# One fused kernel on one core: the experts' down-projection in plain fp32 with tokens on the partitions, and a reordered front and hand-over

## The reference

```python
x = x + xattn0(ln(x), ctx)      # softmax of tri-linear scores, 4 x 256 x 256, then z = [c, a, c*a, c*q2c] @ W_l.T + b_l
x = x + experts(ln(x))          # E = 8 experts, H = 256, top 2 by logits
x = x + xattn1(ln(x), ctx)      # 16 heads of 8, W_q W_k W_v W_o, b_o
x = x + fp8_layer(ln(x))        # rounded to fp8, 128 x 128

def experts(x):
    logits = x @ Wg;  top_vals, top_idx = top_k(logits, 2)
    weights = one_hot(top_idx) * softmax(top_vals)
    for e in range(8):
        u, v = x @ W1[e], x @ W2[e]
        out += ((u * sigmoid(u) * v) @ W3[e]) * weights[..., e]
```

## Time and profile before

| | us |
|---|---|
| median of 3 runs | 230.06 |
| the profiled execution | 230.04 |
| its span, first to last instruction | 228.2 |
| PE, DVE, ACT, POOL busy | 188.1, 167.8, 138.3, 123.9 |
| share of the ending chain: PE, DVE, POOL, ACT, issue | 49%, 13%, 13%, 12%, 9% |
| mean granted PE clock | 0.938 |

### The profile page before, as it was taken

How to read it: one execution, slowest core, us unless ns; L and a number is a source line. 1 busy time by engine, 2 the same in 40 slices (tenths; PEclk the granted TensorE clock), 3 DMA queues, 4 the chain that set the end, 5 groups by cost and what they waited for, 6 DMA issues and landing times.

```text
span 228.2 us, 4007 instructions
## 1 busy us (share of the span) xinstructions
PE 188.1 (82%) x1166; PEld 144.7 (63%) x1166; DVE 167.8 (74%) x408; ACT 138.3 (61%) x273; POOL 123.9 (54%) x141
## 2 busy tenths in 40 slices
PE   5758896795998999999989868789999999886130
PEld 4546795373776788788868657567876887563120
DVE  3775766169697878869874699688988998845764
ACT  2282742974654565645672458988789798665452
POOL 4368464994966999859995246254223232203502
PEclk9999769599999999999999999999999999999755
DMA  6991000000750503203900000000000000000002
GB/s 221 370 408 50 4 0 0 0 0 3 237 134 3 177 10 95 92 0 95 274 0 4 0 0 3 0 0 3 1 4 0 0 0 1 0 3 0 1 0 92
DMA packets 6434, 13.04 MB, mean 57 GB/s; under 512 B 1024, under 2 KB 2048, under 8 KB 6160
## 3 DMA queue, kind: packets, MB, share of 16 engines
q1 hardware_dynamic: 4688, 11.83, 15.3%
q10 hardware_dynamic: 1728, 1.00, 1.4%
HBM read 10.17 MB, written 0.56 MB: 47 GB/s over the span
## 4 chain that ended last, share of the span: by engine, by line
PE 49%; DVE 13%; POOL 13%; ACT 12%; issue 9%; ACTq 2%; DVEq 0%; POOLq 0%
POOL hids L306 7%; PE banks L1353 6%; PE bank L1334 5%; PE bank L1365 5%; PE bank L1106 4%; PE bank L1108 3%; PE bank L1107 3%; PE banks L1106 3%; PE banks L1108 3%; POOL cpT L316 3%; PE banks L1107 3%; DVE negm L973 2%; PE bank L1280 2%; ACT raw L601 2%; POOL att L267 2%
## 5 line engine op out<-in xcount | busy, mean ns | idle before, releaser
L306 POOL TENSOR_TENSOR hids<-attT,hids 128x512 fp32r<-128x512 f32 x32 | 40.9, 1296 | 10.4 <-ACT hids L517 10.2
L973 DVE TENSOR_REDUCE negm<-bank 128x2 f32<-128x512 f32 x64 | 41.9, 687 | 5.3 <-PE bank L1334 3.9
L354 POOL TENSOR_TENSOR wx<-raw,const 32x256 fp32r<-32x256 f32 x32 | 19.5, 608 | 39.3 <-DVE raw L963 32.1
L601 ACT ACTIVATE raw<-banks 128x1024 f32<-128x1024 f32 x32 | 32.5, 1021 | 2.7 <-PE banks L1353 2.4
L517 ACT CAST hids<-attT 128x512 fp32r<-128x512 f32 x32 | 19.9, 621 | 18.7 <-DVE attT L894 10.8
L889 DVE SCALAR_TENSOR_TENSOR att<-att,bank 128x512 f32<-128x512 f32 x32 | 21.9, 684 | 12.0 <-ACT att L511 12.0
L1334 PE MATMUL bank<-wx 128*128 128x512 f32 x64 | 24.9, 430 | 2.0 <-DVE wx L983 1.5
L511 ACT ACTIVATE att<-bank 128x512 f32<-128x512 f32 x32 | 18.8, 594 | 9.2 <-PE banks L1108 7.7
L1106 PE MATMUL bank<-xT,wx 128*128 128x512 f32 x48 | 19.7, 411 | 0.8 <-DVE att L889 0.7
L1108 PE MATMUL bank<-xT,wx 128*128 128x512 f32 x48 | 19.1, 398 | 0.0
L1107 PE MATMUL bank<-xT,wx 128*128 128x512 f32 x48 | 19.0, 396 | 0.0
(11 more groups left out here) (220 smaller groups left out, 463.8 us busy)
## 6 DMA issues: line engine op xcount, KB each, us to landing
rwb<-routing SPq DMA_DIRECT2D x8, 512.0 KB, 4.1
raw<-in_w SPq DMA_DIRECT2D x1, 2048.0 KB, 11.2
wx<-negm SPq DMA_DIRECT2D x1, 2048.0 KB, 8.8
raw<-in_w SPq DMA_DIRECT2D x1, 1024.0 KB, 9.6
xs<-in_x SPq DMA_DIRECT2D x2, 256.0 KB, 3.1
ctxT<-in_ctxT SPq DMA_DIRECT2D x1, 512.0 KB, 5.3
ctx<-in_ctx SPq DMA_DIRECT2D x1, 512.0 KB, 7.1
wl<-in_wl SPq DMA_DIRECT2D x1, 256.0 KB, 7.6
```

The source lines that it names most:

```text
L306: pool.tensor_tensor(hids[:, p, 1, k, :], hid[:, p, k, :], plain(hids[:, p, 0, k, :]), ALU.subtract).then_inc(S["hid_lo"], 1)
L601: act.activation(probs[:, g % 2, 2 * r:2 * r + 2, :, :].rearrange("p h k q -> p (h k q)"), pair[r][:, :], ACT.Exp, scale=ATT_SCALE).then_i ...
L973: dve.tensor_reduce(negm[:, g % 2, r // 2, c0:c0 + QUAD + 1:QUAD], bk[1 + r % 2][:, :].rearrange("p (h k) -> p h k", h=2), AX.X, ALU.max, ...
```

## The change

The experts. `down(n)` uses the hidden tile itself (fp32, not split) as the stationary operand, 128 tokens at a time, and W3 as loaded as the moving operand: eight fp32 products of 128 columns, and the result has tokens on the partitions. So the rounding and the remainder of `hid` go, the split of W3 goes, `weigh` becomes four operations that scale by `rw` (one number for each partition) and add to `xs`, and the accumulation on POOL, the spreading of the routing weights, and both turnings back go. ACT uses Silu in place of tanh, so one DVE product in `hidden` goes; the routing's exp becomes a tanh.

The front. The eight row scalings of the attention are shared by DVE (first tile of a batch) and POOL (second tile, now a tensor_tensor); PE runs 5 + 3 + 3 products with the identity between them (`keep_warm`), and `WARM_UP` is 4. `b_l` is added on POOL ahead of the scalings. `turned(1)` and the copy of `cT` for half 0 go to ACT. z is made by halves: `contexted(0)` stands ahead of `queried(1)`. The normed tiles are made on DVE again, V is projected behind z, half one is turned and `up(0)` starts ahead of the turning of half two and of the logits.

The hand-over. `km` has its own tile and is cleared early; projections 0 and 1 run ahead of `up(14)` and `up(15)` in bank 7; `scores(0, 0, 0)` and `(0, 0, 1)` stand ahead of `down(15)`.

```diff
-WARM_UP = 6
+WARM_UP = 4
@@ transfers (SP)
-            for h in range(2):
-                sp.wait_ge(S["rwT_ev"], h + 1)
-                sp.dma_start(rw_d[:, cols], rwT[:, cols]).then_inc(S["rw_out"], 16)
...
-            sp.wait_ge(S["y_ps"], UNITS - G - 1)
+            sp.wait_ge(S["setup"], 1)
+            sp.wait_ge(S["ld_w12"], 16)
             blank = negm[:, :, :, :]...
@@ POOL
+            for h in range(2):
+                pool.wait_ge(S["ln1"], HALVES[h][1])
+                pool.tensor_tensor(xs[:, tiles, :], xs[:, tiles, :], bl..., ALU.add).then_inc(S["bl_added"], 1)
+            for b in range(BATCH):
+                t = TPB * b + 1
                 pool.wait_ge(S["s_rinv"], b + 1)
-                for t in range(TPB * b, TPB * (b + 1)):
-                    pool.tensor_scalar(att[:, t, :], att[:, t, :], rinv[:, t:t + 1], None, ALU.mult)
+                pool.tensor_tensor(att[:, t, :], att[:, t, :], rinv[:, t:t + 1].broadcast_to([P, SEQ]), ALU.mult)
-            w12_lo(0, 1, 2, 3, 4, 5)
-            negative_mean(0, HALVES[0])
-            w12_lo(6)
-            negative_mean(1, HALVES[1])
-            w12_lo(7)
-            for e in range(0, E, 2):
-                pool.tensor_tensor(w3[:, e:e + 2, 1, :], w3raw[:, e:e + 2, :], plain(w3[:, e:e + 2, 0, :]), ...)
+            w12_lo(0, 1, 2, 3, 4)
+            for h in range(2):
+                inverse_deviation(2, h, HALVES[h])
+            pool.wait_ge(S["ln2"], NT)
+            w12_lo(5, 6, 7)
-            for n in range(2, UNITS):
-                hidden_lo(n)
-                if (n - 2) % E and n - 2 < UNITS - 3:
-                    accumulate(n - 2)
@@ ACT
-                    act.activation(tanhs[:, k, :], bk[2 * k][:, :], ACT.Tanh, scale=0.5).then_inc(S["tanh_s"], 1)
+                    act.activation(silus[:, k, :], bk[2 * k][:, :], ACT.Silu).then_inc(S["silu_s"], 1)
-            def hidden_hi(n, k): ...
+            act.activation(spare[:, :], const[:, C_ZERO:C_ZERO + 1], ACT.Silu)     # ahead of the experts
+            act.activation(spare[:, :], const[:, C_ZERO:C_ZERO + 1], ACT.Exp)      # behind them
@@ DVE
             def inverse_sum(b):
                 ...
+                dve.wait_ge(S["s_rinv"], b + 1)
+                dve.tensor_scalar(att[:, TPB * b, :], att[:, TPB * b, :], rinv[:, TPB * b:TPB * b + 1], None, ALU.mult)
             def hidden(n):
-                    dve.scalar_tensor_tensor(gated[:, k, :], tanhs[:, k, :], 1.0, bk[2 * k][:, :], ALU.add, ALU.mult)
-                    dve.tensor_tensor(hid[:, p, k, :], gated[:, k, :], bk[2 * k + 1][:, :], ALU.mult)
+                    dve.tensor_tensor(hid[:, p, k, :], silus[:, k, :], bk[2 * k + 1][:, :], ALU.mult)
             def weigh(n):
-                dve.tensor_tensor(out, bk[4 + n % 2][:, :], rwb[:, e, :], ALU.mult).then_inc(S["y_w"], 1)
+                for t in range(TPH):
+                    tile = h * TPH + t
+                    ins = dve.scalar_tensor_tensor(xs[:, tile, :], bk[4 + n % 2][:, t * P:(t + 1) * P],
+                                                   rw[:, tile, e:e + 1], xs[:, tile, :], ALU.mult, ALU.add)
+            context_added(0)
+            added_moments(0)
+            context_added(1)
+            scaled(2, 0, HALVES[0])
+            added_moments(1)
+            normed_lo(0)
+            scaled(2, 1, HALVES[1])
@@ PE
+            keep_warm(6, 5)
             attention_turned(0)
+            keep_warm(6, 3)
             attention_turned(1)
+            keep_warm(6, 3)
+            attention_turned(2)
             context_to_query(0)
+            queried(0, range(0, 2))
             (q2c products)
-            queried(0)
+            queried(0, range(2, TPH))
+            contexted(0)
             queried(1)
-            for h in range(2):
-                contexted(h)
+            contexted(1)
             def down(n):
-                for k in range(HB):
-                    ins = three(bk[4 + p][:, :], (w3[:, e, 0, k * P:(k + 1) * P], w3[:, e, 1, k * P:(k + 1) * P]),
-                                (hids[:, p, 0, k, :], hids[:, p, 1, k, :]), k == 0, k == HB - 1)
+                for t in range(TPH):
+                    rows = slice(t * P, (t + 1) * P)
+                    for k in range(HB):
+                        ins = pe.matmul(bk[4 + p][:, rows], hid[:, p, k, rows], w3raw[:, e, k * P:(k + 1) * P],
+                                        start=t == 0 and k == 0, stop=t == TPH - 1 and k == HB - 1)
+            up(0)
+            turn("ln2", "xT_ps", 5, 1)
+            logits(0)
+            up(1, (0,))
+            logits_turned(0)
+            up(1, (1,))
+            for n in range(2, UNITS):
+                if n >= UNITS - 2:
+                    for a in range(2):
+                        project(n - UNITS + 2, n - UNITS + 2, 0, a, bank=7)
+                up(n)
+                ...
+                down(n - 2)
             down(UNITS - 2)
-            project(0, 0, 0, 1, early=True)
-            second_half_part(accT[:, HALF:TOK], first=True)
-            second_half_part(yw3)
-            second_half_part(yw[:, 0, :])
-            down(UNITS - 1)
-            project(0, 0, 0, 0, early=True)
-            second_half_part(yw[:, 1, :], last=True)
             for r in range(2):
                 scores(0, 0, r, True)
+            down(UNITS - 1)
-            for a in range(2):
-                project(1, 1, 0, a)
```

More of the change, by code:

```diff
@@ L193, in build @@
         S = {n: sem(n) for n in names}
-        def added(n):
-            return n - n // E
         block = stack.enter_context(nc.Block())
@@ L1013, in dve_batch @@
                         stack_keys(m + 2, (g + 2) % G, first and g < 2)
-                    if first and g == 0:
-                        add_experts(1)
                     if more:
@@ L1115, in turn, with keep_warm @@
                 ins.then_inc(S[out], 1)
+            def keep_warm(bank, count):
+                for _ in range(count):
+                    pe.matmul(bk[bank][:, 0:P], ident, ident, start=True, stop=True)
             pe.wait_ge(S["setup"], 1)
@@ L1178, in _, with queried @@
             ins.then_inc(S["bcol_ps"], 1)
-            def queried(h):
+            def queried(h, tiles=range(TPH)):
                 pe.wait_ge(S["cc_ev"], h + 1)
-                for t in range(TPH):
+                for t in tiles:
                     tile = h * TPH + t
@@ L1214, in _ @@
                 ins.then_inc(S["v_ps"], 1)
-            for h in range(2):
-                turn("ln2", "xT_ps", 4 + h, h)
+            turn("ln2", "xT_ps", 4, 0)
             def logits(h):
@@ L1268, in down @@
-                ins.then_inc(S["y_ps"], 1)
-            def first_half_turned():
-                pe.wait_ge(S["y_acc"], added(E - 1))
-                for t in range(TPH):
-                    ins = pe.transpose(bk[6][:, t * P:(t + 1) * P], accT[:, t * P:(t + 1) * P], ident)
-                ins.then_inc(S["accT_ps"], 1)
-            def second_half_part(src, first=False, last=False):
-                for t in range(TPH):
-                    ins = pe.matmul(bk[7][:, t * P:(t + 1) * P], src[:, t * P:(t + 1) * P], ident,
-                                    start=first and t == 0, stop=last and t == TPH - 1)
-                if last:
-                    ins.then_inc(S["accT_ps"], 1)
@@ L1306, in project @@
-            def project(m, g, b, a, late=None, early=False):
-                if a == 0 and not early:
+                for t in range(TPH):
+                    rows = slice(t * P, (t + 1) * P)
+                    for k in range(HB):
+                        ins = pe.matmul(bk[4 + p][:, rows], hid[:, p, k, rows], w3raw[:, e, k * P:(k + 1) * P],
+                                        start=t == 0 and k == 0, stop=t == TPH - 1 and k == HB - 1)
+                ins.then_inc(S["y_ps"], 1)
+            def project(m, g, b, a, late=None, bank=0):
+                if a == 0:
```

466 lines of the change are left out of this document (180 added, 286 removed).

## The result

| | before | after |
|---|---|---|
| median, us | 230.56 | 224.66 |
| range of the runs, us | 229.29 to 231.51 | 223.94 to 225.35 |
| profiled execution: span, us | 228.2 | 222.0 |
| mean granted PE clock | 0.938 | 0.954 |

The ratio is 0.973, with a 95% interval of 0.969 to 0.977: 2.7% faster, where 5.5% were forecast. 224.66 lies outside the range of 212.5 to 223.5. The spans differ by 6.2 us, the medians by 5.9.

What follows compares the result with a forecast made beforehand. PE was taken to bound the experts' stage, with waits and half clock ahead of it. Front -10.4, stage +3.5, hand-over -6.3, first batch -0.7 gave -13.9; with 1.3 for the clock, -12.6 on 230.04: 217.4 us, range 212.5 to 223.5.

Steps and rivals of the forecast that it cites:

- The experts' stage: From the end of up(0) to the end of down(14): 71.1 us before, 74.6 after, so +3.5.
- DVE has two products [...] hidden either way: Experts, per unit: DVE's products and scale-and-add operations take 2.5 to 2.8 us in a 4.6 us unit, hidden behind PE.
- The forecast is wrong [...] if DVE rather than PE ends the waits in it: Failure sign for the experts' unit, beside a unit over 5 us, up(0) starting after 39, or half clock over 7 us.
- PE's own price: Experts, per unit: eight fp32 products cost 1.78 us, six removed matmuls save 1.39, returning to fp32r costs 0.09.
- rival "slower": Experts' downs: weight loads not hidden, 3.0 us more a unit, 45 us in all, 262 us; chance 0.04.
- The wait for routing: Experts' stage: one wait of PE for routing, 0.5 us within the 74.6.
- The front: Start to the end of up(0): -10.4 us, from 48.77 to 38.4.
- clock not held: Rival: both half-level clock stretches return, or one in the first 12 us from the shorter warm-up; 222.9 us; chance 0.16.
- lesson of L797: Front, row scalings: DVE's SBUF operations are late beside a POOL tensor_tensor; L797 took 1.14 us where L800 took 0.23.
- The rival made of it: Front, port rival: row scalings wait for each other and delay maxima and copies, +2.6, 220.0 us; chance 0.12.
- Hand-over and batch 0: End of down(14) to turn_maxima: 5.1 us for 11.4, -6.3; second attention's first batch: add_experts leaves DVE, -0.7.
- The clock: Allowance of 1.3 us for a half-level stretch of 6.8 us, with PE waiting around 33 to 35 us.

Runs made afterwards that it cites:

- e1: Changed kernel with three hidden buffers instead of two, so hidden(n) waits for down(n-3); 217.05 us, 0.9405 of the kernel before.
- e8: e1 with the second hidden block left out of every down, four products instead of eight, output incomplete; 208.61 us, one run.
- e3: Changed kernel with WARM_UP 6, as before the change, instead of 4; 223.28 us, 0.9687 of the kernel before.
- e6: e1 with both row scalings of a batch on DVE, none on POOL; 216.07 us, 0.9384 of the kernel before.
- e9: e1 plus WARM_UP 6, both row scalings on DVE and seven identity products in the hand-over; 215.53 us, 0.9358 of the kernel before.
- e2: Changed kernel, still two hidden buffers, with down and weigh one unit behind up instead of two; 217.87 us, 0.9459 of the kernel before.
- e7: e1 with seven identity products in PE's waits of the hand-over; 217.10 us, 0.9421 of the kernel before.
- e10: e9 plus b_l added late on POOL (kv in its own tile) and no keep_warm in the front; 214.69 us, 0.9341 of the kernel before.
- e11: e9 with two hidden buffers and down one unit behind up, in place of three buffers; 214.94 us, 0.9331 of the kernel before.
- e5: e1 with b_l added on POOL behind its row scalings and w12_lo(0), kv in its own tile; 217.86 us, 0.9471 of the kernel before.
- e4: Changed kernel without the eleven keep_warm identity products of the front; 224.16 us, 0.9731 of the kernel before.

## Why the prediction was wrong, step by step

**The experts' stage, the step that failed.** "DVE has two products [...] hidden either way" and "without that cover, DVE's 2.8 would still be below PE" compare amounts of work. They were right as amounts (0.687 and four in 1.12 us) and said nothing on the *place* of the wait. For the stage I added up PE's matmuls and put every wait on DVE at nothing, and I missed that `hidden` had got a new one: `y_ps` moved from the writers of the split copies to DVE's product, and that product frees bank 1 for the next up. With the down two units behind, the two form a circle PE up, DVE product, PE down, each once a unit. The unit was 4.97 us, not 4.64. By e1, nine units by 0.45 and 1.8 of the wait for `norm_lo`, 5.8 us of the stage, and 0.7 of the hand-over hang on it: 6.5 us in all. The profiled execution, 223.94, misses the forecast by the same 6.5; what else went wrong (front 1.7, batch 0 0.9 too little) is about made up by what I had priced too high in the stage (1.5) and held back for the clock (1.3). Between the medians the miss is 7.3, since that execution was the fastest of the four. "The forecast is wrong [...] if DVE rather than PE ends the waits in it" was the right alarm, and it went off: the 0.58 at 80.63 and the 2.05 at 106.70 both end with DVE.

**PE's own price was right, a little high.** The down's sixteen records run from 77.84 to 79.54: 1.70 us, where I had 1.78. Behind them the first two fp32r matmuls start 0.31 us apart instead of 0.23, the 0.09 that I had. With e1 the unit is 4.52 against my 4.64 and the stage 73.1 against 74.6. The four products of the earlier trace rows with their fixed identity were a fair stand-in: weight loads are hidden (rival "slower" falls; e8 gives 0.22 again). The wait for routing, 0.5, didn't show.

**The front, 1.7 us short.** The parts came in (z for half one is added at 30.80 instead of 34.86, at full clock from 13.7 on; up(0) at 37.17 instead of 45.41). Three things in it I had priced at nothing. WARM_UP 4 let the clock fall at 10.3 us on the scores: 1.0 us, by e3. I had it only inside the rival "clock not held". `b_l` on POOL was "while POOL is idle": it was, but DVE wasn't. Its normed tiles took 2.09 beside POOL's 1.26 (0.97 more), and a 128 x 1 sum took 1.26 beside the second addition. I had applied's lesson of L797 to the scalings and not to this tensor_tensor ten lines ahead. And the scalings: shared, they cost DVE 0.81 a batch, where both on DVE take 0.62 (e6).

**Row scalings and the port.** Nothing gained by sharing, as I had it. DVE's 0.81 us from 15.10 ends 0.15 after POOL's 0.61 from 15.15; without POOL one takes about 0.31. The Trainium skill (SBUF — State Buffer, "Who interferes with whom") has a GpSimd operation and a DVE operation in a 2-port mode exclude each other for a whole instruction. This trace agrees in the main: 0.61 and 0.31 in sequence are 0.92, against 0.81 measured; where the 0.11 went, and in which mode DVE's operation ran, it doesn't show. The rival made of it, +2.6 on the end, was too large: with both on DVE, up(0) starts 0.6 us earlier (e9 against e3, both with the longer warm-up) and 0.95 earlier in e6 than in e1.

**Hand-over and batch 0.** -5.6 for -6.3, and 5.00 us against the forecast 5.1 once the buffer is free (e1): the same cause again. (The terms written out for it add up to 4.96.) Batch 0 gave +0.2 for -0.7. In the six profiles with no half-level stretch there (e2, e6, e7, e9, e10, e11), first to fifth maxima take 19.5 us, -0.8 on before, and in the change, e1 and e3 to e5 20.5. So the term was right and the clock took 1.0 back.

**The clock.** I set 1.3 us for one long stretch near 33 to 35 us; two short ones came elsewhere, 1.0 us each. So 2.0 us where I had 1.3, in another place; and keep_warm, on which I had counted, makes no difference that shows (e4), while in e8, which has it, a stretch came at 30 to 33 all the same.

Of the rivals none was the case as a whole. "Clock not held" has with 222.9 the nearest time, and one of its three forms came, a stretch in the first 12 us because of the shorter warm-up, but it cost 1.0 us; the bulk of the miss has another mechanism. I had listed a slower unit only through weight loads, and no rival in which a buffer, not an engine, sets the unit.

## What to carry over

When an intermediate step between a producer and a consumer is taken away, the buffer's wait lands on the producer: look up what else that producer releases, and on which side of it, in the order written out, the buffer's reader stands. Busy shares can't show such a circle; the row to look for is idle time of an engine with ready inputs, ended by the reader of its output. The distance between stages of a pipeline should be chosen anew when a stage falls out: here one unit less did as much as a third buffer of 512 KB.

## What the runs showed that I had not expected

A POOL tensor_tensor slows even tiny DVE operations: L673, a sum of 128 x 1, took 1.26 us beside it, against 0.16 for the same step before, and ended at 11.67 where POOL's ended at 11.66. POOL's tensor_scalar scalings before (0.94 us each) had no such neighbour in DVE's rows that I read.

Leaving out the last stretch of every profile, from 190 us or later to the end, the half-level stretches of the clock came in two lengths: 3.41 us in most kernels, 6.83 in the one before and in e8 from 108.2 us on, and both could come while PE was busy by its own row: the earlier trace rows show busy 1.00 in the windows where the clock fell. Between kernels with four products ahead, which differ in nothing near them, the start varied: e1, e6 and e7 show the clock rising for the first time only at 14.4 to 15.1 us, the change, e2, e4, e5 and e8 at 5.8 to 6.9 and falling again at 9.2 to 10.3, and in e1 the twelve score matmuls took 4.36 us instead of 3.03. Until that first rise the windows print 1.00, though these matmuls ran below full pace; there the distance of the records has to be read, not the clock. A gain of one such stretch, 1.0 us, is visible in a profile and not in a median of four to six executions.
